# Layer 0's prologue in a two-layer attention kernel: who splits K of pair 0, when x chunks and shifts come

## The reference

```
x = x + xattn0(layernorm(x), ctx)        # 16 heads of 8, rotary embedding, softmax
x = x + ffn0(layernorm(x))               # ternary weights, relu
x = x + xattn1(layernorm(x), ctx, mask)  # 16 query heads, 4 key heads, causal and mask
x = x + moe1(x)                          # 8 experts, top 1, gelu
```

## Time and profile before

| what | us |
|---|---|
| median of 3 runs (587.66 to 589.43) | 588.3 |
| profiled execution | 586.95 |
| its span in the profile | 585.1 |
| busy in the span: PE, DVE, ACT, POOL | 495.1, 399.3, 357.0, 374.8 |
| prologue and layer 0's first steps | 0 to 45 |
| rest of layer 0's attention | 45 to about 205 |
| feed-forward, with layer 1's first steps | to about 300 |
| layer 1's attention | to about 480 |
| experts | to 585 |

### The profile page before, as it was taken

One profiled execution on the slowest core, in us unless ns is written; L12 is line 12 of the kernel. 1 busy time (PEld: TensorE's weight loads), 2 busy tenths in 40 slices (PEclk: granted clock), 3 DMA queues, 4 the chain that ended last, 5 costly groups with the idle time before them and its releaser, 6 DMA issues.

```text
span 585.1 us, 20027 instructions
## 1 busy us (share of the span) xinstructions
PE 495.1 (85%) x6238; PEld 363.5 (62%) x6239; DVE 399.3 (68%) x1244; ACT 357.0 (61%) x872; POOL 374.8 (64%) x751
## 2 busy tenths in 40 slices
PE   3569898999988799988799999899998742999993
PEld 2346566666665589986455555555554422999992
DVE  7657777777798568644668888888878763444441
ACT  3227677777766555653566777677765652666661
POOL 6876666667673257675666688878887472445552
PEclk9999999999999999999999999999999985999998
DMA  5734334353432580004443455444554014334430
GB/s 165 184 76 125 90 92 118 85 126 87 119 89 64 193 226 1 1 2 111 118 111 89 104 134 137 128 103 111 133 138 110 26 56 143 80 96 104 101 94 27
DMA packets 102161, 59.92 MB, mean 102 GB/s; under 512 B 20338, under 2 KB 98178, under 8 KB 102098
## 3 DMA queue, kind: packets, MB, share of 16 engines
q1 hardware_dynamic: 98738, 51.79, 35.1%
q0 software_dynamic: 2784, 6.82, 3.4%
q10 hardware_dynamic: 576, 0.53, 0.3%
HBM read 19.90 MB, written 8.81 MB: 49 GB/s over the span
## 4 chain that ended last, share of the span: by engine, by line
PE 47%; SPq 14%; DVE 10%; DMA 10%; issue 10%; ACT 4%; POOL 3%; ACTq 1%; DVEq 0%; POOLq 0%
SPq L395 8%; DMA stack<-pieces 7%; PE bank L847 6%; PE bank L783 5%; PE bank L669 5%; PE scoreT L773 4%; DVE negmax L1408 4%; PE scoreT L835 4%; PE score L613 4%; PE bank L556 2%; PE score L835 2%; SPq L404 2%; PE bank L528 2%; PE scoreT L642 2%; PE bank L684 2%
## 5 line engine op out<-in xcount | busy, mean ns | idle before, releaser
L1408 DVE TENSOR_REDUCE negmax<-score 128x8 f32<-128x1024 f32 x128 | 156.2, 1220 | 35.4 <-PE score L613 24.9
L956 ACT ACTIVATE P<-scoreT 128x1024 f32<-128x1024 f32 x128 | 131.0, 1023 | 40.1 <-PE scoreT L633 21.7
L669 PE MATMUL bank<-P,Vc 128*32 128x128 f32 x2048 | 82.5, 279 | 1.9 <-DVE product L1516 1.5
L613 PE MATMUL score<-stack 64*128 64x128 bf16 x1024 | 62.7, 222 | 22.1 <-DMA stack<-pieces 13.1
L1312 POOL DMA_INDIRECT out<-by x39 | 40.2, 1031 | 50.6 <-DVE by L1715 48.0
L613 PEld LDWEIGHTS score<-stack 64*128 64x128 bf16 x1024 | 33.9, 95 | 48.7 <-issue 22.1
L669 PEld LDWEIGHTS bank<-P,Vc 128*32 128x32 f32 x2048 | 48.4, 109 | 15.8 <-issue 3.6
L962 ACT COPY outs<-bank 128x256 f32<-128x256 f32 x64 | 23.6, 369 | 49.8 <-PE bank L669 49.6
L1176 POOL TENSOR_TENSOR pieces<-full,pieces 128x256 bf16<-128x256 f32 x64 | 42.9, 670 | 14.4 <-ACT pieces L937 14.4
L1179 POOL TENSOR_TENSOR pieces<-rest,pieces 128x256 bf16<-128x256 f32 x64 | 43.8, 685 | 5.0
L847 PE MATMUL bank<-M,bhT 128*128 x312 | 43.5, 282 | 0.3 <-ACT bhT L1082 0.3
(11 more groups left out here) (211 smaller groups left out, 1265.7 us busy)
## 6 DMA issues: line engine op xcount, KB each, us to landing
stack<-pieces SPq DMA_DIRECT2D x192, 128.0 KB, 2.8
ctxT<-in_ctxT SPq DMA_DIRECT2D x32, 128.0 KB, 2.5
XB<-expert_rows SPq DMA_DIRECT2D x39, 66.0 KB
XA<-expert_rows SPq DMA_DIRECT2D x39, 64.0 KB
XR<-in_x SPq DMA_DIRECT2D x4, 512.0 KB, 4.5
stack<-blank SPq DMA_DIRECT2D x32, 64.0 KB, 2.1
stack<-negpT SPq DMA_DIRECT2D x64, 32.0 KB, 1.8
M<-in_M SPq DMA_DIRECT2D x1, 2048.0 KB, 9.9
```

The costliest lines, as they stand in the source:

```text
L613: mm = nc.tensor.matmul(SCORE[:, r, i * 128:(i + 1) * 128], Qs[pb][rows, h, tb * S:(tb + 1) * S], Ks[pb][rows, kv, tb * S:(tb + 1) * S], s ...
L669: mm = nc.tensor.matmul(PVOUT[VCOL * i:VCOL * (i + 1), half * 128:(half + 1) * 128], Vc[:, k % BODY, at:at + VCOL], P32[:, c, i * 128:(i + ...
L956: nc.scalar.activation(P32[:, half * 2:half * 2 + 2, :], SCORET[:], ACT.Exp, scale=SCALE).then_inc(sem("exp_done"), 1)
L1408: nc.vector.tensor_reduce(negmax[:, k % 2, :, half * HQ:(half + 1) * HQ], SCORE[:].rearrange("p r (h k) -> p r h k", h=HQ), AX.X, ALU.max, ...
```

## The change

- K of pair 0 in layer 0 is projected into the first SCORE bank and not into QK, so that it waits for no rotation of Q; PE's next Q projection waits for `q_rotated` and not for `k_rotated`. DVE rotates it from there and then also does POOL's four operations on it (`cut_first_k`); POOL leaves that pair's K out.
- `stack_both`, in all steps of both layers, waits for the high pieces, issues slot 0, waits for the middle pieces, issues slots 1, 2 and 4, waits for the low ones, issues 3 and 5.
- SP issues ctx of pair 1 and x chunk 1 ahead of the other weights, chunk 2 before step -2, chunk 3 before step 1, and the two feed-forward weights F1 and F2 before step 3. `eyeb` moves to the first weights. The waits of PE and ACT for all weights move to where they are first needed.
- GROUPS has four groups of four batches in place of two of eight. DVE does group 3 + t in step t, 0 to 3, before the first reduction of maxima; POOL does group 2 + t in steps 1 to 4, at the step's end after `whole`. Group 2 stands before step -3 on DVE and before -2 on POOL.
- The stack buffers are cleared as float32 words, half as many elements, by POOL ahead of its first group and by DVE all three in the prologue.

```diff
...
 SLOTS = len(QSLOT)
+SLOT_ORDER = (0, 1, 2, 4, 3, 5)
+ONES = float(np.uint32(0x3F803F80).view(np.float32))
 STRIDE = 8
...
 HALF = VCOL // 2
-GROUPS = ((0, 2), (2, 8), (8, 16), (16, 24), (24, 32))
+GROUPS = ((0, 2), (2, 8), (8, 16), (16, 20), (20, 24), (24, 28), (28, 32))
 SCALE = float(1.0 / np.sqrt(np.float32(DK)))
...
             (eye[:], a["eye"]), (W0[:], a["W0"].rearrange("n e m -> e n m")), (cosT[:], a["cosT"]), (sinT[:], a["sinT"]),
+            (eyeb[:], a["eyeb"]),
         ]
...
         other_loads = [
-            (F1[:], a["F1"]), (F2[:], a["F2"].rearrange("(c p) n -> p c n", p=128)), (wgr[:], a["wg"]),
-            (eyeb[:], a["eyeb"]), (negI[:], a["negI"]), (upper[:], a["upper"]),
+            (wgr[:], a["wg"]), (negI[:], a["negI"]), (upper[:], a["upper"]),
             (W1Q[:], a["W1Q"]), (W1K[:], a["W1K"]), (W1V[:], a["W1V"]),
...
         ]
+        late_loads = [(F1[:], a["F1"]), (F2[:], a["F2"].rearrange("(c p) n -> p c n", p=128))]
         expert_loads = [
...
         X_CHUNKS = 4
-        FIRST_LOADED, LOADED, EXPERTS_LOADED = 16 * len(first_loads), 16 * len(other_loads), 16 * len(expert_loads)
+        FIRST_LOADED, LOADED, EXPERTS_LOADED = 16 * len(first_loads), 16 * (len(other_loads) + len(late_loads)), 16 * len(expert_loads)
...
                     if is_pair(p):
-                        cut_q, cut_k = known(3 * (p + P0) + 3), known(3 * (p + P0) + 3)
-
-                        sp.wait_ge(sem("q_pieces"), cut_q)
-                        sp.wait_ge(sem("k_pieces"), cut_k)
-                        for s in range(SLOTS):
+                        high, middle, low = known(p + P0 + 1), known(3 * (p + P0) + 1), known(3 * (p + P0) + 3)
+
+                        sp.wait_ge(sem("q_high"), high)
+                        sp.wait_ge(sem("k_high"), high)
+                        for s in SLOT_ORDER:
+                            if s == SLOT_ORDER[1]:
+                                sp.wait_ge(sem("q_pieces"), middle)
+                                sp.wait_ge(sem("k_pieces"), middle)
+                            if s == SLOT_ORDER[4]:
+                                sp.wait_ge(sem("q_pieces"), low)
+                                sp.wait_ge(sem("k_pieces"), low)
                             sp.dma_start(rows_of(stack[b], s), both_pieces(b, s)).then_inc(sem(f"stacked{L}{b}"), 16)
...
                 run(step, t)
-                if t == -AHEAD + 1:
-                    for dst, src in other_loads:
-                        sp.dma_start(dst, src).then_inc(sem("weights_loaded"), 16)
-                    for c in range(1, X_CHUNKS):
-                        load_x_chunk(c)
+            load_x_chunk(1)
+            for dst, src in other_loads:
+                sp.dma_start(dst, src).then_inc(sem("weights_loaded"), 16)
+
+            def load_late():
+
+                for dst, src in late_loads:
+                    sp.dma_start(dst, src).then_inc(sem("weights_loaded"), 16)
+
             sp.wait_ge(sem("stacks_cleared"), 6)
             sp.wait_ge(sem("zeros_set"), 1)
-            body_loop(sp, step, START)
+            body_loop(sp, step, START, {-2: partial(load_x_chunk, 2), 1: partial(load_x_chunk, 3), 3: load_late})
             for dst, src in expert_loads:
...
             def quantize_sums():
+                pe.wait_ge(sem("weights_loaded"), LOADED)
                 pe.wait_ge(sem("abs_summed"), 2)
...
-                            if L == 0:
+                            if L == 0 and isinstance(p, int) and p == 1:
+                                pe.wait_ge(sem("q_rotated"), 2)
+                            elif L == 0:
                                 pe.wait_ge(sem("k_rotated"), count(2 * p))
...
-                            if L == 0:
+                            if L == 0 and isinstance(p, int) and p == 0:
+                                pass
+                            elif L == 0:
                                 pe.wait_ge(sem("q_rotated"), 2 * p + 2)
...
                                 pe.wait_ge(sem("base_read"), p + 1)
-                        mm = nc.tensor.matmul(QK[:, half * PAIR:(half + 1) * PAIR], W0[:, 3, :] if half else WK, ctxT[b][:],
+                        at = SCORE[:, 0, :] if L == 0 and isinstance(p, int) and p == 0 else QK
+                        mm = nc.tensor.matmul(at[:, half * PAIR:(half + 1) * PAIR], W0[:, 3, :] if half else WK, ctxT[b][:],
                                               start=True, stop=True)
...
                 run(step, t)
-            pe.wait_ge(sem("weights_loaded"), LOADED)
+
             def gate_turn():
...
                 def first_evacs():
+                    act.wait_ge(sem("weights_loaded"), LOADED)
                     evac_xnT(0, 0)
...
                     nc.scalar.copy(Qs[2], blank[:].rearrange("p e w -> p (e w)")[:, 0:HEADS * S // 2].bitcast(BF16).rearrange("p (h s) -> p h s", s=PAIR)).then_inc(sem("stacks_cleared"), 1)
-            act.wait_ge(sem("weights_loaded"), LOADED)
             early = attention(1)
...
                 T0, P0 = L * B, L * PAIRS
+
+                def by_vector(p, which):
+                    return L == 0 and which == 1 and isinstance(p, int) and p == 0
+
                 def whole(k, which):
...
                     p = pair(k)
-                    if is_pair(p):
+                    if is_pair(p) and not by_vector(p, which):
                         nm = "qk"[which]
...
                     p = pair(k)
-                    if is_pair(p):
+                    if is_pair(p) and not by_vector(p, which):
                         nm = "qk"[which]
...
                             whole(j + 5, 1)
+                        if isinstance(t, int) and 1 <= t <= 4:
+                            x_group(2 + t)
                     if L:
...
             step = attention(0)
+            for i in range(2):
+                nc.gpsimd.memset(stack[i][:].bitcast(F32)[:, :, 0, :], 0.0).then_inc(sem("stacks_cleared"), 1)
             x_group(0)
             x_group(1)
-            for i in range(2):
-                nc.gpsimd.memset(Qs[i], 0.0).then_inc(sem("stacks_cleared"), 1)
             for t in range(-AHEAD, START):
...
-            body_loop(pool, step, START, {-3: partial(x_group, 2), -2: partial(x_group, 3), -1: partial(x_group, 4),
+            body_loop(pool, step, START, {-2: partial(x_group, 2),
                                           B - 7: gate_norm,
...
                     dve.wait_ge(sem(f"{nm}_full"), count(p + P0))
+                    first_k = L == 0 and which == 1 and isinstance(p, int) and p == 0
+                    at = SCORE[:, 0, :] if first_k else QK
                     for tab, dst, off in ((cosT, rotA, 0), (sinT, rotB, PAIR)):
...
                             dst[which][:].rearrange("p (b s) -> p b s", b=2),
-                            QK[:, off:off + PAIR].rearrange("p (b s) -> p b s", b=2),
+                            at[:, off:off + PAIR].rearrange("p (b s) -> p b s", b=2),
                             tab[:].unsqueeze(1).broadcast_to([128, 2, 128]), ALU.mult)
                         ins.then_inc(sem(f"{nm}_rotated"), 1)
+                    if first_k:
+                        cut_first_k()
+
+                def cut_first_k():
+
+                    h, f, r = pieces[0][:, 3, :], full[1][:], rest[1][:]
+                    dve.wait_ge(sem("k_rotated"), 2)
+                    nc.vector.tensor_tensor(f, rotA[1][:], rotB[1][:], ALU.add).then_inc(sem("k_full"), 1)
+                    dve.wait_ge(sem("k_high"), 1)
+                    nc.vector.tensor_tensor(pieces[0][:, 4, :], f, h, ALU.subtract).then_inc(sem("k_pieces"), 1)
+                    nc.vector.tensor_tensor(r, f, h, ALU.subtract).then_inc(sem("k_pieces"), 1)
+                    dve.wait_ge(sem("k_pieces"), 2)
+                    nc.vector.tensor_tensor(pieces[0][:, 5, :], r, pieces[0][:, 4, :], ALU.subtract).then_inc(sem("k_pieces"), 1)
...
                     add_out(t - 3, j - 3)
+                    if L == 0 and isinstance(t, int) and 0 <= t <= 3:
+                        x_group(3 + t)
                     if L and t > B and j % 2 == 1:
...
-            def last_groups():
-
-                x_group(3)
-                x_group(4)
-
             step = attention(0)
             def clear(i):
-                nc.vector.memset(Ks[i], 1.0).then_inc(sem("stacks_cleared"), 1)
+                nc.vector.memset(stack[i][:].bitcast(F32)[:, :, 1, :], ONES).then_inc(sem("stacks_cleared"), 1)
...
             x_group(1)
-            clear(0)
-            clear(1)
+            for i in range(3):
+                clear(i)
             dve.wait_ge(sem("first_loaded"), FIRST_LOADED)
...
                 run(step, t)
-                if t == -AHEAD + 2:
-                    clear(2)
             dve.wait_ge(sem("zeros_set"), 1)
...
             early = attention(1)
-            begin, rest = ffn(early, {0: bias_ones, 1: bias_first, 2: bias_rest, 3: bias_second, 4: bias_again, 5: bias_last,
```

(5 more changed lines are left out.)

## The result

The changed kernel takes 581.25 us (578.9 to 582.88, 4 runs) where the kernel before, on the same chip, takes 588.87 (587.66 to 589.98, 4 runs): 0.9868 of its time, 95% interval 0.9825 to 0.9911. Forecast was 586.4, range 583.0 to 590.5. Three more comparisons on other chips gave 581.35, 579.31 and 582.62 (0.9888, 0.9850, 0.9894). So the kernel is 5.6 to 9.5 us faster by the medians, not 2, and the range missed it on the fast side. The ratios leave out executions that took over 1.5% more than the fastest of their kernel, so they need not be the quotient of the two medians.

A forecast was written before the change was run, and what follows sets the result against it. It saw SyncE's six slots and their flight leading the chain, and GpSimd ending last in the prologue. Terms -6.4 + 3.6 + 1.4 - 0.5 = -1.9 us on the 588.3 median gave 586.4 us, range 583.0 to 590.5.

The forecast's parts named there:

- +1.4 - 0.5: SyncE's stack_both: added waits and a register value cost 1.4 us over 13 stacks; finer waits give back 0.5.
- The prologue, -6.4: Before step 0, GpSimd's line gets shorter, so batch 0's maxima split starts at 27.6, not 34.08: 6.4 us earlier.
- The bound of 7.3: Upper bound of the prologue's gain, if the 0.95 us is also saved a second time at VectorE.
- VectorE beside GpSimd: Prologue: VectorE's four K operations beside GpSimd's three on Q; no slowdown, or one 0.67 us wait each, staying hidden.
- The give-back, 3.6: Steps 1 to 4: GpSimd's shift groups delay the maxima's transpose and TensorE, losing 3.6 us; bounds 1.0 and 6.5.
- its upper bound of 3.6: Most that SyncE's longer stack_both was said to cost in the 13 stacks where the ring decides; lower bound 0.6.
- The clock: TensorE's clock rise was assumed to come 6 us earlier with the work; otherwise up to 2.5 us more.
- The shifts find room: Rival, chance 0.2: the shift groups in the steps give back only 1.0 us, total 583.8 us.
- SP's queue longer in every pair: Rival, chance 0.14: at 0.1 per wait, 0.45 per stack, +9.9 us over about 22 pairs; 594.9 at worst.
- its point of slower: Extra SyncE time per stack, about 0.31 us, from which that rival makes the kernel slower by 0.3%.
- its low edge: Bottom of the forecast range, 583.0 us, taken from the low edge of the rival that the shifts find room.
- a ring: Scores, maxima's transpose, ACT's copy, SP's copy, six slots, flight, scores; elsewhere hidden by a little behind VectorE's reduction.

The follow-up runs named there:

- the two kernels without them: Changed kernel with its late shift groups left out (582.27 us, 0.9894); changed kernel with shifts in groups of eight ahead of step 0 (586.43 us, 0.9962).
- the kernel without groups: Changed kernel without shift groups 3 to 6 in steps 0 to 4 on GpSimd and VectorE, batches 16 to 31 unshifted: 582.27 us, 0.9894.

## Why the prediction was wrong

The step that failed is SyncE's: the prediction counted the new `stack_both` as +1.4 - 0.5 = +0.9 us, and the runs show -1.7 (alone) to -2.9 (in the changed kernel). Two more terms, the prologue and the give-back, had the right sign and were sized too slow by 1.1 us and by 0.4 to 1.3, so that all three errors lie on the same side.

- **The prologue, -6.4: right in mechanism, 1.1 short.** GpSimd's line set it, as the shifts put back show (6.2 us). Of the 1.06 missing, 0.84 lie at the split (26.76, not 27.6): 0.41 is the start of Q's cut (18.89, not 19.3), and 0.43 are gaps that I counted and GpSimd has not (7.87 us for what I put at 8.3). The rest is 0.08 of rounding (34.08 - 27.6 is 6.48) and 0.14 at the projection behind the split, 1.90 for 2.04. The start of Q's cut came out near by luck: I had it follow ScalarE's normalising, which stands at 16.21 to 17.09, well ahead. What it follows is VectorE, whose rotation of Q starts at 16.82, right behind its work on K and 1.4 us after the projection's end (14.26 + 1.20). With K back on GpSimd the cut of Q starts at 16.95. The bound of 7.3 was passed by 0.02 at the split. Stack 0, issued from 15.24, was hidden as said, and TensorE no longer waits for ctx 1.
- **VectorE beside GpSimd.** The step held both bounds open; the rows at 15.34 and 15.55 show 0.89 for an operation of 0.42 and 0.82 for one of 0.67. The Trainium skill, page SBUF — State Buffer, section Who interferes with whom, says that a VectorE instruction with two inputs in SBUF contends with a GpSimd one that reads SBUF; the trace agrees, with both lengthened in part. It was not hidden as said: K's pieces were in time, but the rotation of Q stood behind them on VectorE, ahead of GpSimd's line.
- **The give-back, 3.6: right place, near in size.** 2.34 in the first profile, 3.0 to 3.2 in three more. Four stalls in front of the transpose came as forecast, 3.9 us in place of 5.2, since the transpose waits 1.14 and not 1.3 of a group's 1.92 in three steps, and 0.46 in the one that has waited for a stack. Waits for a stack absorb 2.4, where the step had 1.9. What the step missed: the groups aren't the only thing there. In the two kernels without them a stack is late in one long wait and TensorE's clock falls (2.42 us and 0.50; 2.6 and 0.76), and 3.8 and 2.1 us are given back all the same. How much of the changed kernel's give-back is the groups' own stays open.
- **SyncE, +1.4 - 0.5: the term with the wrong sign.** Its price per stack held (0.1 us), though its upper bound of 3.6 is not worked out (0.45 on 13 stacks would be 5.9). But the term was a price of instructions alone. It never priced the order of the slots, which the change also alters, and took the gain of finer waits from the one wait of SP that the earlier trace rows showed. The old and the new form beside each other differ by 2.9 us, against +0.9. Of that, 2.0 to 2.6 is seen in layer 1; how it divides between order and waits is not settled. Another part lies in layer 0, where the first scores stand 2.5 us earlier by it (23.55 against 21.08), the split of batch 0's maxima 1.0 to 1.4 and the scores of batch 2 0.1 to 1.4, less where the projection between them met the high clock (1.10 for 2.04). Why a stack lands sooner by it stays open.
- **The clock.** I assumed TensorE's rise moves with the work. It did, by more than one amount: the first projection at 1.03 us in the regular steps is at 38.95, not 46.88, and the one at 33 us takes 2.02 here and 1.10 in three of the other kernels. In between the rows differ from before in both directions: granted 0.50 from 30 to 35 us, and two projections at 14.26 and 17.71 at the high level. The Trainium skill, page TensorE: Matmul & The Clock Gate, Part 1, says that idling lowers the clock; the profile of the kernel without groups agrees (2.42 us of waiting, then 0.50).
- **The rivals.** "The shifts find room" was nearest in time (583.8) and wrong in reason: they found none, 3.9 us of stalls. "SP's queue longer in every pair" is refuted in price (0.02 per wait, not 0.1) and confirmed in leverage: 0.2 us a stack went with 3 to 6 us. I put its point of slower at 0.31 a stack, so I knew how sharp this edge is, and used it on one side only.

The range failed by the same step: its low edge had no case in which the change to SyncE's loop gains.

## What to carry to other kernels

Where a ring is hidden by little in every period, price an edit of it with both signs, and count every part of the edit, order included: 0.1 to 0.2 us per period went with 2 to 6 us here. Background work put into the steps belongs behind the operation that the critical engine waits for, not ahead of it: same work, 3.9 us of stalls or none, though the time that this won is not clear of noise. And before a lead of one execution is put down to an edit, look at the duration of the same matmuls: here 1.0 us of it was the clock.

## What the runs showed of the hardware

The executions of one kernel differ by 6 us and more, and a part of that is TensorE's clock between the layers. The stretch from the first scores of layer 1 to its batch 6 takes 33.0 to 33.9 us in five profiles (before among them) and 35.4 to 37.7 in the fifteen others, with the same work. Four of the five keep a granted clock of 1.00 from 265 to 290 us; the fifth is the changed kernel's first profile, with one short fall. The windows show it and the last profile of the same kernel:

```profile
277.00:281.00 4.00, 4.00 (x39) 1.82 (x38) 2.36 (x4) 2.82 (x6) 2.04 (x3) 0.57 0.14 29
```

```profile
277.75:281.75 4.00, 4.00 (x23) 1.96 (x19) 2.28 (x3) 1.58 (x3) 2.05 (x3) 0.50 0.08 16
```

In the last, the window ahead of it is granted 0.77 already and the one behind 0.88, where the first profile has 1.00 on both sides. TensorE had been busy 2.81 us of 4 just before, and 2.86 in the first. So nearly the same work sees the clock fall earlier or later, or not at all, for 1.7 us and more. No experiment tried to hold it up there.

That the order in which six DMAs of 128 KB are issued changes their median time to landing by 0.1 to 0.2 us (2.8 to 2.6 in the kernel before, 2.7 to 2.6 in the changed one with the old waits in layer 0) I had not expected either.
